# A graph attention stage rebuilt on groups of 32 nodes, with scores and sums on TensorE

## The reference

```python
xl = (x @ W_l).reshape(N, 4, 64);  xr = (x @ W_r).reshape(N, 4, 64)   # x is layer-normed
e = xl[src] + xr[dst]
e = where(e >= 0, e, 0.2 * e)
score = einsum('ehd,hd->eh', e, att)
ex = exp(score - segment_max(score, dst)[dst])
alpha = ex / (segment_sum(ex, dst)[dst] + 1e-16)
agg = segment_sum(alpha[:, :, None] * xl[src], dst)
h = elu(agg + bias) + x;  graph = layernorm(h) * gamma + beta
# then: 64 experts 256 -> 512 -> 256 with relu, the 2 best of a router's logits per node
```

## Time and profile before

| what | us |
|---|---|
| median of three executions | 866.19 |
| span of the profiled execution | 870.6 |
| first tile's expansion begins | 51.4 |
| last tile's expansion | 587.9 |
| first matmul of the route phase | 623.1 |
| busy: TensorE, VectorE, ScalarE, GpSimd | 721.0, 560.3, 355.9, 411.5 |

### The profile page before, as it was taken

How to read it: one execution, slowest core, us unless ns; L and a number is a source line. 1 busy time by engine, 2 the same in 40 slices (tenths; PEclk the granted TensorE clock), 3 DMA queues, 4 the chain that set the end, 5 groups by cost and what they waited for, 6 DMA issues and landing times. The chain is left out here.

```text
span 870.6 us, 14203 instructions
## 1 busy us (share of the span) xinstructions
PE 721.0 (83%) x4151; PEld 490.7 (56%) x4153; DVE 560.3 (64%) x1355; ACT 355.9 (41%) x1256; POOL 411.5 (47%) x405
## 2 busy tenths in 40 slices
PE   4844777997999889988988898998855499999995
PEld 2722444665666666666766565776544255555553
DVE  5653657886778777777876687878697333434333
ACT  1411334554455555555554464657632121121220
POOL 0566666366667656666765566710326011212121
PEclk9975798999999999999998899999955699999998
DMA  4545463344354435353534353510299899999995
GB/s 122 98 156 148 111 170 97 113 114 125 94 150 112 135 90 149 100 144 95 156 95 125 97 139 108 133 30 1 93 411 405 249 317 367 367 369 370 368 390 200
DMA packets 66875, 154.81 MB, mean 178 GB/s; under 512 B 17390, under 2 KB 30142, under 8 KB 66769
## 3 DMA queue, kind: packets, MB, share of 16 engines
q1 hardware_dynamic: 45824, 100.40, 34.2%
q0 software_dynamic: 18384, 51.06, 21.5%
q10 hardware_dynamic: 2592, 2.43, 0.9%
HBM read 138.76 MB, written 15.39 MB: 177 GB/s over the span
## 5 line engine op out<-in xcount | busy, mean ns | idle before, releaser
L131 POOL DMA_INDIRECT G<-xl_tab,srcI x324 | 344.6, 1064 | 196.0 <-issue 80.4
L783 ACT ACTIVATE L<-psE 128x264 f32<-128x264 f32 x324 | 126.4, 390 | 277.6 <-PE psE L696 200.0
L696 PE MATMUL psE<-G,ident 128*128 128x264 f32 x648 | 209.2, 406 | 0.0
L707 PE MATMUL agg<-msg,M 128*128 128x256 f32 x648 | 191.2, 395 | 6.4 <-issue 4.8
L693 PE MATMUL psE<-xr,MT 128*128 x972 | 176.9, 292 | 0.0
L854 DVE TENSOR_TENSOR L<-L,attb 128x792 f32<-128x792 f32 x108 | 105.7, 978 | 93.6 <-ACT M L784 46.5
L689 PE MATMUL psE<-identb,MT 128*128 128x128 bf16 x324 | 74.1, 229 | 81.4 <-issue 39.2
L805 ACT ACTIVATE msg<-G,A 128x64 f32<-128x64 f32 x432 | 136.8, 354 | 1.5 <-PE agg L707 1.2
L707 PEld LDWEIGHTS agg<-msg,M 128*128 128x128 f32 x648 | 118.5, 194 | 33.3 <-issue 17.4
L693 PEld LDWEIGHTS psE<-xr,MT 128*128 128x128 bf16 x972 | 88.5, 101 | 41.7 <-issue 6.0
L696 PEld LDWEIGHTS psE<-G,ident 128*128 128x128 f32 x648 | 105.5, 203 | 5.1
(11 more groups left out here) (302 smaller groups left out, 723.1 us busy)
## 6 DMA issues: line engine op xcount, KB each, us to landing
w<-in_L_ffn_W SPq DMA_DIRECT2D x120, 512.0 KB
relb<-rel_d SPq DMA_DIRECT2D x36, 288.0 KB
G<-xl_tab,srcI POOLq DMA_INDIRECT x324
tabs<-tab_d SPq DMA_DIRECT2D x48, 98.2 KB
X<-xs_d SPq DMA_DIRECT2D x58, 64.5 KB
xn<-in_L_ffn_W SPq DMA_DIRECT2D x6, 512.0 KB
h_in<-in_L_ffn_W SPq DMA_DIRECT2D x6, 512.0 KB
xs_d<-zslot SPq DMA_DIRECT2D x8, 322.5 KB
```

The costliest lines, as they stand in the source:

```text
L131: nc.gpsimd.indirect_dma_start(out=G[:, g % RG, u * DX:(u + 1) * DX], out_offset=None, in_=xl_tab, in_offset=bass.IndirectOffsetOnAxis(ap= ...
L696: nc.tensor.matmul(psE[:, e, 0:DX], ident[:, :], G[:, s % RG, u * DX:(u + 1) * DX], start=False, stop=True).then_inc(expanded, 1)
L707: last = nc.tensor.matmul(agg[:, bass.ds(w * D, D)], M[:, s % RM, u * P:(u + 1) * P], msg[:, s % RA, u * D:(u + 1) * D], start=False, stop ...
L783: nc.scalar.activation(L[s % RL][:, u * DX:(u + 1) * DX], psE[:, e, 0:DX], ACT.Relu)
```

## The change

The graph phase is written anew, with the same arithmetic otherwise ordered.

- A window has 32 nodes, so there are 40 windows and up to 352 tiles; U = 4 tiles are a step, there are 88 steps, and 7 steps are a block, of which there are 13. LAG is 13, and `G` has 20 slots of 4 tiles.
- The features lie in the partitions. `expand` makes, for each half of the features, `xr3.T @ MT` in one bf16 product (the three parts of 32 nodes lie below each other in the partitions, so one product sums them) and adds `G.T` by a product with the identity. Each is 128 x 128.
- ScalarE takes two tiles at once out of PSUM, as relu and as a plain copy.
- The scores are products on TensorE (`score`): the attention weights are a stationary matrix of 32 columns, and the four tiles of a step go to four column tiles of the array, 16 products of 128 columns per step. They land as rows, so the block's scans read PSUM directly.
- Only the maximum is scanned. The exponential `X` is used as it is; a column of ones in `xl_tab`, between the heads, makes the aggregation also sum the denominators. The division is done once per node at the start of the route phase.
- VectorE's `weigh` makes `M`, the weights put in place of the ones of a 128 x (4 heads x 32 nodes) matrix; TensorE's `aggregate` makes 16 products per step with 32 stationary columns and 66 moving ones, one column tile per head, into `psA`; VectorE's `accumulate` adds each tile's 128 x 66 result into `acc` in SBUF, at an address read from a register.
- In the node phase `xr3` must be laid out anew: SyncE issues 60 DMAs of 32 x 2 x 256 elements, in the last place of its node phase list.

In the orders below `MATMUL` is one call (x16: sixteen alike), `ISA` a register operation and `TENSOR_LOAD` a load of registers.

The core of the diff:

```diff
-DX = HEADS * HX
 NW = -(-N // P)
 NREM = N - (NW - 1) * P
 NPAD = NW * P
+WN = P // HEADS
+NV = NPAD // WN
+QV = NV // NW
+PARTS = 3
 TILES = -(-E // P)
-U = 3
-B = 27
-NI = -(-(TILES + NW - 1) // B) * B
+U = 4
+GPB = P // (U * HEADS) - 1
+B = GPB * U
+STEPS = -(-(TILES + NV - 1) // U)
+NB = -(-STEPS // GPB)
+NI = NB * B
+BJ = B + U
 RB = HEADS * BJ
-CH = 3
+CH = 4
 CI = NI // CH
-assert B % U == 0 and NI % CH == 0 and CI <= P and RB <= P
-STEPS = NI // U
+assert NI % CH == 0 and CI <= P and RB == P and U * WN == P
...
 RING = 18
-RG, GS, AHEAD = 26, 8, 3
-LAG = 20
-RM, RT, RL, RA = LAG + 2, 4, 3, 4
+RG, GS, AHEAD = 20, 8, 3
+LAG = 13
+RM, RT, RL, RE = 4, 4, 3, 3
 LEAD = 2
...
+            for i in range(NW // 2):
+                sp.wait_ge(xr_set, i + 1)
+                for j in range(PARTS):
+                    for r in range(QV):
+                        sp.dma_start(xr3_of[j * WN:(j + 1) * WN, 2 * i:2 * i + 2, r, :], parts[r * WN:(r + 1) * WN, 2 * i:2 * i + 2, j, :]
+                                     ).then_inc(xr3_in[(i + 1) // 2], 16)
...
                 if GS <= s < RG:
                     g.wait_ge(consumed, s - GS + 1)
+                if s == AHEAD + 3:
+                    for k in range(NW // 4 + 1):
+                        g.wait_ge(xr3_in[k], 16 * PARTS * QV * min(k + 1, 2))
                 if s == RG - MG:
-                    g.wait_ge(marks_out, 16 * 7)
+                    g.wait_ge(rel_ps, 1)
+                    g.wait_ge(marks_out, 16 * 4)
+                    g.wait_ge(tab_out, 16 * TOUT)
                 if s >= RG:
-                    g.wait_ge(freed, s - RG + 2)
+                    g.wait_ge(agged, s - RG + 1)
                 gather_group(nc, G, xl_tab, srcI, gathered, s)
...
             def expand(s, u, w):
 
-                i, e = s * U + u, (s * U + u) % 2
+                i, n, e = s * U + u, (s * U + u) // 2, (s * U + u) // 2 % RE
                 if u == 0:
                     pe.wait_ge(onehot, s + 1)
-                if i >= 2:
-                    pe.wait_ge(evacuated, i - 1)
-                mt = MT[s % RT][:, u * P:(u + 1) * P]
-                turned = nc.tensor.matmul(psE[:, e, DX:DX + P], mt, identb[:, :], start=True, stop=True)
-                if u == 1:
-                    turned.then_inc(consumed, 1)
-                for j in range(3):
-                    nc.tensor.matmul(psE[:, e, 0:DX], mt, xr3[:, bass.ds(w * (3 * DX) + j * DX, DX)], start=(j == 0), stop=False)
-                if u == 0:
-                    pe.wait_ge(gathered[s % GS], 16 * U * (s // GS + 1))
-                nc.tensor.matmul(psE[:, e, 0:DX], ident[:, :], G[:, s % RG, u * DX:(u + 1) * DX], start=False, stop=True
-                                 ).then_inc(expanded, 1)
-
-            def aggregate(s, u, w):
-
-                if u == 0:
-                    pe.wait_ge(weighted, s + 1)
-                    if s % GPB == 0 and s > 0:
-                        pe.wait_ge(rescaled, s // GPB)
-                if u == U - 1:
-                    pe.wait_ge(shared, s + 1)
-                last = nc.tensor.matmul(agg[:, bass.ds(w * D, D)], M[:, s % RM, u * P:(u + 1) * P],
-                                        msg[:, s % RA, u * D:(u + 1) * D], start=False, stop=False, skip_group_check=True)
-                if u == 0:
-                    last.then_inc(freed, 1)
-                if u == U - 1:
-                    last.then_inc(agged, 1)
-
+                if i % 2 == 0 and n >= RE:
+                    pe.wait_ge(evacuated, 2 * (n - RE + 1))
+                if i % (2 * QV) == 0 and i < NV:
+                    k = (i // (2 * QV) + 1) // 2
+                    pe.wait_ge(xr3_in[k], 16 * PARTS * QV * min(k + 1, 2))
+                for c in range(KC):
+                    to = psE[:, e, (i % 2 * KC + c) * P:(i % 2 * KC + c + 1) * P]
+                    spread = nc.tensor.matmul(to, xr3[:, bass.ds(w * D + c * P, P)], MT[s % RT][:, u * P:(u + 1) * P], start=True, stop=False)
+                    if (u, c) == (1, 0):
+                        spread.then_inc(consumed, 1)
+                    if (u, c) == (0, 0):
+                        pe.wait_ge(gathered[s % GS], 16 * U * (s // GS + 1))
+                    at = u * DX + c * CX + 1
+                    last = nc.tensor.matmul(to, G[:, s % RG, at:at + P], ident[:, :], start=False, stop=True)
+                if i % 2 == 1:
+                    last.then_inc(expanded, 1)
+
+            def score(s):
+
+                b, k = s // GPB, s % GPB
+                pe.wait_ge(evacuated, 4 * (s + 1))
+                if k == 0 and b >= 2:
+                    pe.wait_ge(ends_set, b - 1)
+                at = WN - HEADS * (k + 2)
+                for j in range(2):
+                    for c in range(KC):
+                        for u in range(U):
+                            last = nc.tensor.matmul(psS[u * WN:(u + 1) * WN, b % 2, 0:P], attz[:, j, c, at:at + WN], L[s % RL][:, j, u, c, :],
+                                                    start=(k == 0 and c == 0 and j == 0), stop=(s + 1 == block_end(b) and c == KC - 1 and j == 1),
+                                                    skip_group_check=True)
+                last.then_inc(scored, 1)
+
+            def aggregate(s):
+
+                pe.wait_ge(weighted, s + 1)
+                if s >= 2:
+                    pe.wait_ge(acced, U * (s - 1))
+                for u in range(U):
+                    for h in range(HEADS):
+                        at = u * DX + h // 2 * CX + h % 2 * HD
+                        last = nc.tensor.matmul(psA[h * WN:(h + 1) * WN, s % 2, u * HX:(u + 1) * HX],
+                                                M[:, s % RM, u * P + h * WN:u * P + (h + 1) * WN],
+                                                G[:, s % RG, at:at + HX], start=True, stop=True)
+                last.then_inc(agged, 1)
...
+                if 1 <= s <= STEPS:
+                    score(s - 1)
+                if s >= LAG:
+                    aggregate(s - LAG)
...
-            def evacuate(s, u):
-
-                i, e = s * U + u, (s * U + u) % 2
-                act.wait_ge(expanded, i + 1)
-                if u == 0 and s >= RL:
+            def evacuate(s, half):
+
+                n = 2 * s + half
+                act.wait_ge(expanded, n + 1)
+                if half == 0 and s >= RL:
                     act.wait_ge(scored, s - RL + 1)
-                if u == 0 and s >= RM:
-                    act.wait_ge(agged, s - RM + 1)
-                if (s, u) == (RM - TS - LS, 0):
-                    act.wait_ge(tab_out, 16 * (NB + 1))
-                nc.scalar.activation(L[s % RL][:, u * DX:(u + 1) * DX], psE[:, e, 0:DX], ACT.Relu)
-                nc.scalar.copy(M[:, s % RM, u * P:(u + 1) * P], psE[:, e, DX:DX + P]).then_inc(evacuated, 1)
+                for j, of in enumerate((ACT.Relu, ACT.Copy)):
+                    nc.scalar.activation(L[s % RL][:, j, 2 * half:2 * half + 2, :, :], psE[:, n % RE, :].rearrange("p (u c e) -> p u c e", u=2, c=KC),
+                                         of).then_inc(evacuated, 1)
...
-            def attend(s):
-
-                dve.wait_ge(evacuated, U * (s + 1))
-                every = L[s % RL][:, :].rearrange("p (u f) -> p u f", u=U)
-                V.tensor_tensor(every, every, attb[:, :].unsqueeze(1).broadcast_to([P, U, DX]), ALU.mult).then_inc(att_mul, 1)
-
-            def score(s):
+                    c(V.tensor_scalar(begins[:, b % 3, 0:1], part[:, 0:1], prow32[:, 0:1], None, ALU.is_equal))
+                    c(V.tensor_scalar(begins[:, b % 3, 1:2], part[:, 0:1], prow32[:, 0:1], None, ALU.not_equal))
+                V.tensor_scalar(MT[s % RT][:, :], part, prow32[:, 0:1], None, ALU.is_equal).then_inc(onehot, 1)
+
+            def weigh(s, u):
 
                 b, k = s // GPB, s % GPB
-                dve.wait_ge(att_mul, s + 1)
-                if k == 0 and b >= 2:
-                    dve.wait_ge(scores_ps, b - 1)
-                V.tensor_reduce(S[:, b % 2, :, 1 + k * U:1 + (k + 1) * U].rearrange("p h u -> p u h"),
-                                L[s % RL][:, :].rearrange("p (u h f) -> p u h f", u=U, h=HEADS), AX_X, ALU.add).then_inc(scored, 1)
-
-            def weight(s):
-
-                b, k, n = s // GPB, s % GPB, U - 1
-                if k == 0:
+                if u == 0 and k == 0:
                     dve.wait_ge(alpha_set, b + 1)
-                if s >= RA:
-                    dve.wait_ge(agged, s - RA + 1)
-                V.tensor_tensor(msg[:, s % RA, 0:n * D].rearrange("p (q d) -> p q d", d=HD),
-                                G[:, s % RG, 0:n * DX].rearrange("p (q f) -> p q f", f=HX)[:, :, 0:HD],
-                                A[:, b % 2, k * U:k * U + n, :].rearrange("p u h -> p (u h)").unsqueeze(2)
-                                .broadcast_to([P, n * HEADS, HD]), ALU.mult).then_inc(weighted, 1)
-
-            def rescale(b):
-
-                dve.wait_ge(agged, GPB * b)
```

(53 more changed lines are left out.)

592 lines of the change are left out of this document (273 added, 319 removed).

## The result

The change made the kernel slower by 15%. After takes 992.92 us (four runs, 990.79 to 994.74), before 864.64 us on the same chip (four runs, 862.23 to 868.87): ratio 1.149, 95% interval 1.143 to 1.155. The forecast was 825 us, with 778 to 888 as its range.

The account below looks back on a forecast made before the run. GpSimd's gathers were taken to bound the new kernel at 5.46 us a step: 870.6 us profiled, less 45 for an earlier route phase, plus 4 within it, 829.6; without the profile's 4.4 us excess, 825 us, range 778 to 888.

Parts of the forecast that it names:

- What bounds the kernel before: Graph phase before: TensorE bounds at 77% of a 4.97 us step, the other 1.16 us waits in ping-pong with ScalarE.
- TensorE's step, 3.83 to 5.12 us beside GpSimd's 5.46: Graph phase, step of four tiles: TensorE needs 3.83 us with four column tiles at once, 5.12 with two, both below GpSimd.
- they hide TensorE's 3.83 to 5.12: Graph phase: GpSimd's gathers set the pace, 5.46 us for four tiles, with TensorE's, VectorE's and ScalarE's work hidden beside them.
- GpSimd's pace, 1.366 us a gather: Graph phase: a gather with its gap takes 1.366 us on average, 1.24 at best; four make a step of 5.46.
- Rival A: Graph phase: gathers run at their best pace of 1.24 us, 42 us less, 783 us in all; chance 0.20.
- Rival B: Graph phase: TensorE's small load-and-matmul pairs run at a fixed 0.065 us, step 6.70, 946 us in all; chance 0.14.
- the estimate of 928 us: Graph phase: at the skill page's about 62 ns per MATMUL without hardware decoding, step 6.5 us and about 928 us.
- Rival C: Graph phase: round-trip waits between TensorE, ScalarE and VectorE return, step 5.8 to 6.0 us, 875 us; chance 0.16.
- The start, 74 us: Before the graph phase: 60 DMA issues at 0.45 us, 27 us, after 44, plus 3 for the barrier; begins at 74, not 51.
- The tail, 34 us: End of graph phase: 14 steps without expansion, VectorE slowest at 2.4 us each, together 34 us.
- The route phase, +4 us: Route phase: VectorE's new sums and reciprocal, about 2 us, and 80 products on column tiles, 4.3 us mostly hidden; adds 4.
- the forecast's mechanism: Graph phase: GpSimd's gathers set a step of 5.4 to 5.5 us, 800 to 845 us in all; chance 0.50.

Follow-up runs that it names:

- held chip: Kind of chip, not an edit: the kernel before takes 859, 871 and 863 us on three; after unchanged, run again on two, 1001.7 and 993.9 us.
- free chip: Kind of chip, not an edit: the kernel before takes 779 and 775 us on two; after unchanged was not run there.
- variants of after: After with gathers of rows 0 to 127, with gathers of 52 numbers a row, or with half the score products left out: 822.5 to 824.1 us.

## Why the prediction was wrong

**What bounds the kernel before: wrong, and the root of the rest.** I read 1.16 us of waits per step as a ping-pong of TensorE and ScalarE. They came with the indirect gathers: with plain loads the step is 3.92 us, near the 3.81 that I had counted for TensorE undisturbed, although ScalarE waits for TensorE as before (200.0 us in 537.6, and 160.9 in 418 now). In the run with plain loads:

```profile
POOL G L131 <- PE agg L705: 201.5, 81, 13.3
ACT L L781 <- PE psE L694: 160.9, 297, 12.4
```

The waits of before had a line that I passed over, TensorE idle for "issue":

```profile
PE psE L689 <- issue: 39.2, 23, 6.7
```

An engine that is idle for up to 6.7 us with nothing to wait for was what had to be explained.

**TensorE's step, 3.83 to 5.12 us beside GpSimd's 5.46: the step that failed.** As a sum of work it was inside its two ends: 4.44 us measured without the hold, 0.61 above the likelier 3.83. Scores and sums take 1.35 us (I took four at a time, 1.29). The expansion takes 0.334 us for each pair of products, 2.67 a step and not 2.19, as the fp32 product of 128 columns takes 0.28 us to the next start (690.57 to 690.85) and not 128/264 of 0.44. But in the place where it runs, the step is 6.73 us. The step of the prediction that failed is the overlap, "they hide TensorE's 3.83 to 5.12": I let GpSimd's and TensorE's work lie side by side. On a held chip they do not: the last of 88 steps of expansions comes 605.6 us after the first where I had 469. Of the 136.6 us too little, 55 are in the first 20 steps (164 us where I had 20 x 5.46 = 109, and 85 with plain loads): there, trains of 28 and 24 gathers made one step 35 and one 28 us long, and the granted clock was 0.68 from 100 to 200 us (1.00 with plain loads). Why GpSimd's indirect transfers hold TensorE stays open.

**GpSimd's pace, 1.366 us a gather: pessimistic.** 1.25 in a train, 1.27 on average on a free chip (5.08 us a step). Rival A had the pace right and the bound wrong.

**Rival B**, TensorE's small pairs at a fixed pace of 0.065 us, gave 6.70 us a step and 946 us. Its step agrees with the 6.73 and its reason is refuted: without the gathers a pair of the sums takes 0.46/32 = 0.014 us. The Trainium skill (TensorE: Matmul & The Clock Gate, "Wait — 56ns, not 53.3ns?") gives its 62 ns for each MATMUL for the case that the hardware does not decode. These 14 ns show that this bound is not in force here, so the estimate of 928 us from it does not apply. A time that comes out near is no proof of its cause. **Rival C**, waits that come back, named engines that were idle (VectorE 41% busy, ScalarE 27%).

**The start, 74 us: mis-sized, 91.8.** The mechanism was right (60 issues, then the barrier), and halving the list on one queue took 20 us off. An issue took 0.68 us and not 0.45; 0.59 stood in the earlier trace rows as the other reading, and the list began at 49 and not 44.

**The tail, 34 us: right**, 35.0. **The route phase, +4 us: mis-sized, +12.** VectorE's sums and division hold the first product until 735.11, and then TensorE, busy for 15.5 of the last 32 us of the tail, runs at 1.2 GHz. The windows of the tail and of the route products:

```profile
700.00:732.00 32.00, 15.49 (x457) 12.40 (x446) 26.37 (x121) 0.57 (x2) 0.00 (x0) 0.59 0.01 3
...
735.00:754.50 19.50, 19.39 (x171) 9.49 (x171) 8.45 (x25) 3.85 (x7) 3.53 (x3) 0.50 0.99 387
```

The granted clock is 0.50 over the 19.3 us that these products take, for 5.1 us of the group that they replace. With the later start this is 17 us more; what follows is 5 us shorter than before (237.5 for 242.5).

**On a free chip** the forecast's mechanism holds: GpSimd sets a step of 5.08 us, and variants of after take 822 to 824 us where I said 825. That nearness is luck: the 340 gathers were forecast some 30 us too long (1.27 us each and not 1.366), the start 18 us and the route phase 8 us too short, and these nearly cancel. And there the kernel before takes 777 and not 866, as it is free of the hold too, so even there the sign was wrong: slower by 6%.

## What to carry to other kernels

Idle time of TensorE under "issue" is a finding, not noise: look at what another engine does at its begin and its end, above all GpSimd with indirect transfers, before summing engines as if they ran side by side. Replacing the gathers by plain loads of the same bytes is a cheap run that shows a kernel's time without the hold, and it would have shown here that before had 110 us to win in a place that this change does not touch. Compare kernels on one chip only, and look at the time of the kernel before in each comparison: on two of the five chips the effect hardly shows.
